# One core, sixteen batches in a pipeline: a layer norm moved one period on, tanh issued behind the gate matmul, a piece of A on GpSimd, A^T and B^T turned by DMA

## Chip, core and metric

The kernel runs on one core of one Trainium2 chip. The metric is the device time of one execution in microseconds, and the number that counts is the median of several executions. The engines are TensorE (PE, its weight loads are listed as PEld), VectorE (DVE), ScalarE (ACT), GpSimd (POOL) and SyncE (SP), which in this kernel only issues DMAs.

## The reference

The input x has 16 batches of 256 tokens of 128 features. One transformer layer is computed: an attention over a window of 128 tokens with 16 heads of 8 features, then a gated feed-forward part whose operands are rounded to a 4-bit grid in blocks of 16, each with a residual and a layer norm.

```
g = x @ Wg.T + bg ;  v = x @ Wv.T + bv                  # 16 heads of 8
corr = (g_i . g_j) / (|g_i| |g_j| + 1e-8) * m           # m: window mask
corr = (corr + 1) / 2
denom = mean_j(corr) + 0.5
fitness = 1 / (denom * sum_i(1 / denom))
attn = softmax(corr * fitness_i, masked)
x = layernorm(x + (attn @ v) @ Wo.T + bo)
gate, up = q(x) @ q(w_gate).T, q(x) @ q(w_up).T         # q: to a 4-bit grid, blocks of 16
h = silu(gate) * up
x = layernorm(x + q(h) @ q(w_down).T)
```

## The kernel before

All five engines run programs written out by hand, each a loop over a period number t from -3 to 20. The engines meet by semaphores only, and each engine takes its instructions strictly in the order written. In one period t every engine does a piece of work for several batches: the genes and values of batch t+3, the normalised genes and the fitness of batches t+2 and t+1, the scores and exponentials of batch t, the rest of its attention with t-1, the first layer norm and the rounding of x of batch t-2, the gate, up and hidden part of t-2 and t-3, and the down projection and second layer norm of t-4.

Scores of a batch come from two half-precision matrices. A16 holds the normalised genes gh in four pieces per head: the rounded value twice and the remainder (the low piece) twice; B16 holds the genes times fitness (Bf) in the same way. Both lie with tokens on the 128 partitions and must be turned so that the pieces lie on partitions; the results are AT and BT, two buffers each.

- GpSimd writes the rounded halves of B16 (L516) and A16 (L525), VectorE the low halves: `low_B` (L1175) and, for A, L1344.
- TensorE turns them with `turn16` (L811), eight 128x128 transposes through PSUM bank WB for each matrix, and ScalarE copies the bank to AT (L617) and BT (L635).
- `scores` (L745, L751) of eight pairs of heads fill PSUM banks S; ScalarE's `exps` (L568) empty them; a pair waits for the exponentials of the pair before. `values` (L772) multiplies the result with v.
- `window_sums` (L847) needs A16 complete, and gives VectorE the row sums (L1377 to L1390, the last of them `rden`); `fitness_sums` (L858) sums `rden` on TensorE, and `project` (L796) follows it there.
- `gate_up` (L804, L805) multiplies first for the gate, then for the up part. `tanh` on ScalarE (L599) waits for the semaphore that the up matmul raises; VectorE then does `gate` (L1181) and `up` (L1187).
- The second layer norm of batch t-4 is made in period t: `residual_2` (L1168) and the statistics `st2` (L1148) and `mv2` (L1154) on VectorE between the rounding steps `hm` (L1199), `rstd` on GpSimd (L501 to L506) between its two products `hq` (L495), the result `yo` on ScalarE (L574) at the end of the period.
- `newton` on GpSimd (L471 to L478) finds 1/|g| in twelve small steps at the start of its period; the first layer norm's `rstd` follows behind B16's copy.
- SP issues per period one load of x turned (L378), one load of x (L382) and one store (L385), 128 KB each.

## Time and profile before

| what | value |
|---|---|
| median of 3 executions | 354.0 us (353.38 to 361.8) |
| the profiled execution | 353.57 us |
| its span in the trace | 351.9 us |
| busy: PE, DVE, ACT, POOL | 280.9, 266.8, 236.8, 176.2 us |
| mean granted TensorE clock | 0.935 |

The profiled execution stands for the runs. 1.67 us of it lie outside the span, ahead of the first instruction and behind the last. No engine is busy all the time, so the page's table of busy shares alone doesn't say what sets the time; the chain of work that ended last and the engines' own lists in order of time do.

### The profile page before, as it was taken

To read this page: it belongs to the slowest core of one execution; us is meant where nothing else is said; L and a number is where in the kernel's file an instruction comes from. 1 tells how busy PE (TensorE), PEld (TensorE's weight loads), DVE (VectorE), ACT (ScalarE), POOL (GpSimd) and SP (SyncE) were. 2 spreads that over 40 slices of the span, in tenths; PEclk is the share of its full clock that TensorE was granted. 3 is DMA by queue.
4 is the path that set the end of the run, shared out by engine and by line. 5 is a ranking of instruction groups with operands and counts; after the bars stand their busy time and mean duration, and the time that the engine had idled before them with its cause. 6 is when DMAs were issued, how large, how long until landed. Compare 5 with 4: busy or idle time off the path is not lost.

```text
span 351.9 us, 13497 instructions
## 1 busy us (share of the span) xinstructions
PE 280.9 (80%) x5268; PEld 190.1 (54%) x5268; DVE 266.8 (76%) x777; ACT 236.8 (67%) x531; POOL 176.2 (50%) x457
## 2 busy tenths in 40 slices
PE   5548788887898989898989898889888989762731
PEld 3334455655565656565656565657564656531521
DVE  3752856578989798989888888989898989867631
ACT  2044655777787979797979797979796988531330
POOL 6463330626455656566565656565655244351351
PEclk9999955999999999999999999999999999986765
DMA  4100000101010101011010101010001010000000
GB/s 129 30 3 31 17 4 1 34 2 34 5 30 12 40 14 37 16 35 30 21 32 21 31 18 35 17 33 2 23 13 32 5 34 4 15 10 4 19 15 19
DMA packets 12422, 7.93 MB, mean 23 GB/s; under 512 B 1026, under 2 KB 12356, under 8 KB 12356
## 3 DMA queue, kind: packets, MB, share of 16 engines
q1 hardware_dynamic: 12356, 7.03, 7.0%
q8 instruction: 43, 0.70, 0.8%
q14 instruction: 23, 0.19, 0.2%
HBM read 4.93 MB, written 2.10 MB: 20 GB/s over the span
## 4 chain that ended last, share of the span: by engine, by line
DVE 34%; PE 30%; issue 17%; ACT 9%; POOL 8%; DMA 1%; SPq 0%; POOLq 0%; ACTq 0%; DVEq 0%
PE OT L772 8%; ACT Pm L568 4%; PE WC L804 3%; DVE xn L1230 3%; PE WB L811 3%; DVE hm L1199 3%; PE WA L823 2%; PE S L745 2%; PE WD L805 2%; DVE A L1344 2%; ACT y L574 2%; DVE st L1148 2%; PE WB L796 2%; DVE xn L1238 2%; DVE xn L1240 2%
## 5 line engine op out<-in xcount | busy, mean ns | idle before, releaser
L568 ACT ACTIVATE Pm<-S 128x384 f32<-128x384 f32 x256 | 111.4, 490 | 36.2 <-PE S L751 36.2
L772 PE MATMUL OT<-Pm,gv 128*32 128x256 f32 (+1 forms) x1024 | 58.0, 346 | 0.0
L495 POOL TENSOR_TENSOR hq<-hm,hs 128x352 f32<-128x352 f32 x32 | 25.6, 801 | 62.7 <-DVE hm L1199 62.7
L745 PE MATMUL S<-BT,AT 32*32 32x160 f16 (+4 forms) x2048 | 40.7, 223 | 14.9 <-ACT Pm L568 13.7
L745 PEld LDWEIGHTS S<-BT,AT 32*32 32x32 f16 x2048 | 17.8, 88 | 46.8 <-ACT Pm L568 32.0
L772 PEld LDWEIGHTS OT<-Pm,gv 128*32 128x32 f32 x1024 | 27.6, 113 | 20.9 <-issue 6.2
L804 PE MATMUL WC<-wguT,xaT 128*128 128x352 f32 x58 | 26.3, 536 | 6.6 <-ACT xaT L656 6.2
L751 PE MATMUL S<-mask,ident 32*32 32x96 f16 x1024 | 31.1, 206 | 0.0
L912 PE MATMUL WD<-wdT,hqT 128*128 128x128 f32 (+1 forms) x192 | 26.8, 292 | 1.8 <-ACT hqT L628 1.8
L1181 DVE SCALAR_TENSOR_TENSOR hh<-th,WC 128x352 f32<-128x352 f32 x29 | 14.5, 499 | 17.4 <-ACT th L599 17.4
L588 ACT ACTIVATE hu<-hn,off 128x352 f32<-128x352 f32 x32 | 18.8, 591 | 12.5 <-POOL hn L489 12.5
L912 PEld LDWEIGHTS WD<-wdT,hqT 128*128 128x128 f32 (+1 forms) x192 | 23.8, 199 | 3.4 <-ACT hqT L628 2.4
L489 POOL TENSOR_TENSOR hn<-h,hrn 128x352 f32<-128x352 f32 x32 | 24.7, 793 | 1.3
L1199 DVE SCALAR_TENSOR_TENSOR hm<-hu,hn 128x352 f32<-128x352 f32 x32 | 22.0, 687 | 3.7 <-ACT hu L588 3.7
L823 PE MATMUL WA<-wgv,xT 128*128 128x256 f32 x64 | 21.5, 469 | 4.0 <-DMA bgrow<-bg_dram 3.8
L599 ACT ACTIVATE th<-WC 128x352 f32<-128x352 f32 x29 | 13.4, 463 | 16.6 <-PE WD L805 16.6
L805 PE MATMUL WD<-wguT,xaT 128*128 128x352 f32 x58 | 23.1, 482 | 0.0
L504 POOL TENSOR_TENSOR rstd<-ve,mhalf 128x2 f32<-128x2 f32 x32 | 22.9, 715 | 0.0
L574 ACT ACTIVATE yo<-y,nb,rstd 128x128 f32<-128x128 f32 x32 | 14.0, 489 | 10.7 <-POOL nb L506 10.7
L617 ACT ACTIVATE AT<-WB 128x1024 f16<-128x1024 f16 x16 | 16.4, 1023 | 6.9 <-PE WB L811 5.7
L501 POOL TENSOR_SCALAR ve<-mv 128x2 f32<-128x2 f32 x32 | 9.8, 306 | 20.3 <-DVE mv L1154 19.0
L471 POOL TENSOR_TENSOR nt<-seed 128x32 f32<-128x32 f32 x15 | 4.0, 265 | 28.1 <-DVE seed L1116 28.1
(165 smaller groups left out, 694.7 us busy)
## 6 DMA issues: line engine op xcount, KB each, us to landing
xT<-x_turned_dram SPq DMA_DIRECT2D x16, 128.0 KB, 2.3
x_res<-x_dram SPq DMA_DIRECT2D x16, 128.0 KB, 2.2
out_dram<-yo SPq DMA_DIRECT2D x16, 128.0 KB, 2.1
wf<-w_down_dram SPq DMA_DIRECT2D x1, 176.0 KB, 2.5
wgv<-wgv_dram SPq DMA_DIRECT2D x1, 128.0 KB
wf<-w_gate_dram SPq DMA_DIRECT2D x1, 128.0 KB, 2.1
wf<-w_up_dram SPq DMA_DIRECT2D x1, 128.0 KB, 2.1
woT<-wo_dram SPq DMA_DIRECT2D x1, 64.0 KB
```

The lines of the kernel that those rows point to most:

```text
L489: pool.tensor_tensor(b3(hn[:, k]), b3(h[:, k]), bc(hrn[:, k], QB), ALU.mult).then_inc(s_hn, 1)
L495: pool.tensor_tensor(b3(hq[:, k, 0:I]), b3(hm[:, k]), bc(hs[:, k], QB), ALU.mult).then_inc(s_hq, 1)
L504: pool.tensor_tensor(r[:, :], ve[:, :], mhalf[:, 0:NT], ALU.pow).then_inc(s_out, 1)
L568: act.activation(Pm[:, group % PR, hd % 4, :], S[:, (H * x + hd) % 3, 0:SCW], ACT.Exp, scale=1.0 / ZS).then_inc(s_exp, 1)
L745: pe.matmul(S[k0:k0 + KG, bank, at:at + n], AT[r:r + 32, x % 2, c, q:q + KG], BT[r:r + 32, x % 2, c, q:q + n], start=(kt == 0), stop=False)
L751: i = pe.matmul(S[k0:k0 + KG, bank, 0:SCW].rearrange("p (b c) -> p b c", c=P)[:, :, k0:k0 + KG], ident16[m:m + KG, m:m + KG], near[m:m + K ...
L772: i = pe.matmul(OT[VP * g:VP * (g + 1), T - (q1 - q0):T], gv_flat[:, at:at + VP], Pm[:, (GROUPS * x + c) % PR, g, q0:q1], start=(kt == 0 a ...
L804: pe.matmul(g, lhs, wguT[:, 0:I], start=True, stop=True)
L805: pe.matmul(u, lhs, wguT[:, I:2 * I], start=True, stop=True).then_inc(s_gu, 1)
L823: pe.matmul(WA[:, k * 2 * D:(k + 1) * 2 * D], xT[:, (t + 3) % 2, k * P:(k + 1) * P], wgv[:, :], start=(k == 0), stop=False)
L912: i = pe.matmul(WD[:, k * D:(k + 1) * D], hqT[0:kn, k, n * P:(n + 1) * P], wdT[0:kn, n, :], start=(n == 0), stop=(n == 2))
L1199: dve.scalar_tensor_tensor(out=hm[:, k], in0=hu[:, k], scalar=ROUND, in1=hm[:, k] if step else hn[:, k], op0=ALU.max, op1=op).then_inc(s_h ...
```

## The change

Four things are changed. The second layer norm's statistics, `rstd` and result of batch x are now made in period x+5 for the batches below 12 (`late`); `residual_2` stays in period x+4, and y2 has two buffers. `tanh` waits for a new semaphore that the gate matmul raises, and `up` waits for the up matmul's own. A's low piece is computed by GpSimd, after the two products `hn` and ahead of the moved `rstd`. `turn16` and the two ScalarE copies are gone: SP issues for each of A and B two transposing DMAs from SBUF to SBUF, 128x512 half-precision elements each, behind the low piece and the end of the scores that read the same buffer. TensorE's `scores` wait for the DMA's semaphores, and so do GpSimd's writes of the next A16 and B16.

```diff
-        y2 = sb("y2", [P, NT, D])
+        y2 = sb("y2", [P, 2, NT, D])
...
+        def late(x):
+
+            return x < B - 4
...
+            def turned(src, dst, x, s_done):
+
+                for n in range(NT):
+                    sp.dma_start(dst[:, x % 2, :, n * P:(n + 1) * P],
+                                 src[:, n * H:(n + 1) * H].rearrange("p h r d -> p (h r d)"),
+                                 transpose=True).then_inc(s_done, 16)
...
+                for x in (t - 6, t - 5):
+                    if live(x) and late(x) == (x == t - 6):
+                        sp.wait_ge(s_yo, NT * x + NT)
+                        sp.dma_start(ov[x], yo[:, x % 2]).then_inc(st_o[x % 2], 16)
+
+                if live(t + 1):
+
+                    need(sp, s_sc, H * t)
+                    sp.wait_ge(s_Blo, t + 2)
+                    turned(B16, BT, t + 1, s_B)
+                if live(t + 2):
+
+                    need(sp, s_sc, H * (t + 1))
+                    sp.wait_ge(s_Alo, t + 3)
+                    turned(A16, AT, t + 2, s_A)
...
-                    need(pool, s_A, t + 2)
+                    need(pool, s_A, 32 * (t + 2))
                     pool.tensor_copy(A16[:, :, 0:2, :], twice(gh)).then_inc(s_Ahi, 1)
...
                 if live(t - 3):
                     h_over_scale(t - 3, 0)
                     h_over_scale(t - 3, 1)
+                if live(t + 2):
+
+                    pool.wait_ge(s_Ahi, t + 3)
+                    pool.tensor_tensor(A16[:, :, 2:4, :], twice(gh), A16[:, :, 0:2, :], ALU.subtract).then_inc(s_Alo, 1)
+                if live(t - 5) and late(t - 5):
+                    norm_2(t - 5)
+                if live(t - 3):
                     h_times_scale(t - 3, 0)
...
             def tanh(x, k):
-                act.wait_ge(s_gu, NT * x + k + 1)
+                act.wait_ge(s_gate, NT * x + k + 1)
...
-                if live(t + 1):
-                    act.wait_ge(s_A, t + 2)
-                    need(act, s_sc, H * t)
-                    act.activation(AT[:, (t + 1) % 2].rearrange("p c t -> p (c t)"), WB16, ACT.Copy).then_inc(s_AT, 1)
...
                 if p == 0:
-                    pe.wait_ge(s_AT, x + 1)
-                    pe.wait_ge(s_BT, x + 1)
+                    pe.wait_ge(s_A, 32 * (x + 1))
+                    pe.wait_ge(s_B, 32 * (x + 1))
...
-                pe.matmul(g, lhs, wguT[:, 0:I], start=True, stop=True)
+                pe.matmul(g, lhs, wguT[:, 0:I], start=True, stop=True).then_inc(s_gate, 1)
...
+                if live(t - 5) and late(t - 5):
+                    sums_2(t - 5)
+                    aggr_2(t - 5)
                 if live(t - 3):
                     gate(t - 3, 1)
...
-                if live(t + 2):
-                    dve.wait_ge(s_Ahi, t + 3)
-                    need(dve, s_A, t + 2)
-                    dve.tensor_tensor(A16[:, :, 2:4, :], twice(gh), A16[:, :, 0:2, :], ALU.subtract).then_inc(s_Alo, 1)
```

GpSimd, from A's rounded halves (`A<-gh`) over the hidden part's products `hn` and `hq` to the first step of the next period's `newton` (`nt<-seed`), in the kernel before:

```order
L525 CAST A<-gh 128x32x16
L485 TENSOR_SCALAR hrn<-hr 128x44
L489 TENSOR_TENSOR hn<-h,hrn 128x352 x2
L495 TENSOR_TENSOR hq<-hm,hs 128x352
L501 TENSOR_SCALAR ve<-mv 128x2
L502 TENSOR_SCALAR nm<-mv 128x2
L504 TENSOR_TENSOR rstd<-ve,mhalf 128x2
L506 TENSOR_TENSOR nb<-nm,rstd 128x2
L495 TENSOR_TENSOR hq<-hm,hs 128x352
L471 TENSOR_TENSOR nt<-seed 128x32
```

The same place in the changed kernel:

```order
L551 CAST A<-gh 128x32x16
L506 TENSOR_SCALAR hrn<-hr 128x44
L510 TENSOR_TENSOR hn<-h,hrn 128x352 x2
L562 TENSOR_TENSOR A<-gh,A 128x32x16
L522 TENSOR_SCALAR ve<-mv 128x2
L523 TENSOR_SCALAR nm<-mv 128x2
L525 TENSOR_TENSOR rstd<-ve,mhalf 128x2
L527 TENSOR_TENSOR nb<-nm,rstd 128x2
L516 TENSOR_TENSOR hq<-hm,hs 128x352 x2
L492 TENSOR_TENSOR nt<-seed 128x32
```

The four steps of `rstd` moved ahead of both `hq`, A's low piece is new ahead of them, and the two `hq` now stand together.

VectorE, from the last step of rounding x (`xm`) over A's low piece, the rounding of the hidden part (`hm`) and the second norm (`y<-y,WD`, `st`, `mv`) to the sizes of the genes (`n`), in the kernel before:

```order
L1243 TENSOR_TENSOR xm<-xn,xs 128x256
L1344 TENSOR_TENSOR A<-gh,A 128x32x16
L1199 SCALAR_TENSOR_TENSOR hm<-hu,hn 128x352
L1168 TENSOR_TENSOR y<-y,WD 128x256
L1199 SCALAR_TENSOR_TENSOR hm<-hu,hm 128x352
L1148 BN_STATS st<-y 128x6 x2
L1199 SCALAR_TENSOR_TENSOR hm<-hu,hn 128x352
L1154 BN_AGGR mv<-st 128x2 x2
L1199 SCALAR_TENSOR_TENSOR hm<-hu,hm 128x352
L1110 TENSOR_REDUCE n<-gsq 128x32
```

The same place in the changed kernel:

```order
L1263 TENSOR_TENSOR xm<-xn,xs 128x256
L1219 SCALAR_TENSOR_TENSOR hm<-hu,hn 128x352
L1187 TENSOR_TENSOR y<-y,WD 128x256
L1219 SCALAR_TENSOR_TENSOR hm<-hu,hm 128x352
L1219 SCALAR_TENSOR_TENSOR hm<-hu,hn 128x352
L1219 SCALAR_TENSOR_TENSOR hm<-hu,hm 128x352
L1122 TENSOR_REDUCE n<-gsq 128x32
```

A's low piece left this engine, and the second norm's `st` and `mv` left this stretch; for the batch before they now stand earlier in the period, between `Bf` and the second `gate`.

ScalarE, from the copy of the values (`OTs`) to the first layer norm's result (`y`), in the kernel before:

```order
L599 ACTIVATE th<-WC 128x352
L568 ACTIVATE Pm<-S 128x384 x2
L581 ACTIVATE OTs<-OT 128x256
L617 ACTIVATE AT<-WB 128x1024
L568 ACTIVATE Pm<-S 128x384 x2
L574 ACTIVATE y<-y,nb,rstd 128x128 x2
```

The same place in the changed kernel:

```order
L637 ACTIVATE th<-WC 128x352
L601 ACTIVATE Pm<-S 128x384 x2
L614 ACTIVATE OTs<-OT 128x256
L601 ACTIVATE Pm<-S 128x384 x2
L607 ACTIVATE y<-y,nb,rstd 128x128 x2
```

The copy of AT left the line between the exponentials; the copy of BT, later in the period, left it in the same way.

## Rows read from the trace of the kernel before

**Rows 1.** Chain that ended last, in order of time: start us, us, what; whole trace.

```profile
93.56 0.36 DVE rden L1390
...
185.67 0.57 PE WB L811 x8
...
187.18 0.87 ACT Pm L568 x2
...
193.00 0.68 DVE A L1344
...
198.06 0.36 DVE rden L1390
...
267.51 0.36 DVE rden L1390
```

**Rows 2.** ScalarE's instructions: start us, us, line, [idle before <-who ended it], one period.

```profile
184.64 0.46 ACT L599 ACTIVATE th<-WC 128x352 f32<-128x352 f32 x1 [0.40 <-PE WD L805]
...
185.79 0.39 ACT L581 ACTIVATE OTs<-OT 128x256 f32<-128x256 f32 x1
...
188.03 0.88 ACT L574 ACTIVATE y<-y,nb,rstd 128x128 f32<-128x128 f32 x2
```

**Rows 3.** GpSimd's instructions, same columns and period.

```profile
187.95 0.61 POOL L525 CAST A<-gh 128x512 f16<-128x512 f32 x1
...
194.96 0.79 POOL L495 TENSOR_TENSOR hq<-hm,hs 128x352 f32<-128x352 f32 x1 [4.48 <-DVE hm L1199]
196.45 0.30 POOL L501 TENSOR_SCALAR ve<-mv 128x2 f32<-128x2 f32 x1 [0.70 <-DVE mv L1154]
...
197.91 0.79 POOL L495 TENSOR_TENSOR hq<-hm,hs 128x352 f32<-128x352 f32 x1
198.66 0.24 POOL L471 TENSOR_TENSOR nt<-seed 128x32 f32<-128x32 f32 x1
```

**Rows 4.** VectorE's instructions, same columns and period.

```profile
185.14 0.52 DVE L1181 SCALAR_TENSOR_TENSOR hh<-th,WC 128x352 f32<-128x352 f32 x1 [1.08 <-ACT th L599]
...
193.60 0.52 DVE L1199 SCALAR_TENSOR_TENSOR hm<-hu,hn 128x352 f32<-128x352 f32 x1
...
194.80 0.48 DVE L1148 BATCH_NORM_STATS2 st<-y 128x6 f32<-128x128 f32 x2
195.19 0.94 DVE L1199 SCALAR_TENSOR_TENSOR hm<-hu,hn 128x352 f32<-128x352 f32 x1
196.05 0.23 DVE L1154 BATCH_NORM_AGGREGATE mv<-st 128x2 f32<-128x6 f32 x2
...
197.73 0.17 DVE L1116 TENSOR_SCALAR seed<-seed 128x32 int32<-128x32 int32 x1
```

**Rows 5.** TensorE's matmuls, same columns and period.

```profile
193.22 0.41 PE L937 MATMUL WC<-identf,xm 128*128 128x128 f32 x2 [0.38 <-DVE xm L1243]
...
197.44 0.23 PE L751 MATMUL S<-mask,ident 32*32 32x96 f16 x8
198.56 0.38 PE L858 MATMUL WA<-rden,onesf 128*128 128x32 f32 x2 [0.89 <-DVE rden L1390]
```

**Rows 6.** SP's loads of x, line 382: times of issue (min/median/max ns), landing.

```profile
L382 SPq DMA_DIRECT2D x_res<-x_dram x16: 367/368/441, 12.4 to 286.9; - x16
...
DMA to landing us min/median/max: 2.0/2.2/3.5
```

**Rows 7.** DMA queue, page part 3: packets, MB, share of 16 engines.

```profile
q1 hardware_dynamic: 12356, 7.03, 7.0%
```

**Rows 8.** Start of the kernel, instructions of VectorE, TensorE and GpSimd.

```profile
20.78 0.85 DVE L1344 TENSOR_TENSOR A<-gh,A 128x512 f16<-128x512 f32 x1 [0.71 <-POOL A L525]
...
22.53 0.82 PE L847 MATMUL WB<-A,win 128*128 128x128 f16 x6
...
24.70 0.75 POOL L441 MEMSET gv<- 128x782 f32 x1
```

**Rows 9.** Busy us by engine in a stretch: PE, PEld, DVE, ACT, POOL, granted clock, DMA.

```profile
40.00:60.00 20.00, 15.75 (x291) 10.24 (x291) 12.68 (x25) 10.58 (x23) 4.95 (x15) 0.57 0.01 3
```

More of the change, by code:

```diff
@@ L188, in layer @@
         WD = ps("WD", [P, 512])
-        WB16 = WB[:, :].bitcast(F16)
         ld_w = sem("ld_w")
@@ L234, in layer @@
         s_xqT = sem("s_xqT")
+        s_gate = sem("s_gate")
         s_gu = sem("s_gu")
@@ L506, in rstd, with norm_2 @@
                 pool.tensor_tensor(nb[:, :], nm[:, :], r[:, :], ALU.mult).then_inc(s_out, 1)
+            def norm_2(x):
+                need(pool, s_yo, NT * x)
+                rstd(x, mv2, ve2, rstd2, nm2, nb2, s_ln2, 5 * x + 5, s_rs2)
             for t in range(FIRST, LAST + 1):
@@ L535, in _ @@
                     rstd(B - 1, mv1, ve1, rstd1, nm1, nb1, s_ln1, 5 * B, s_rs1)
-                if live(t - 4):
-                    rstd(t - 4, mv2, ve2, rstd2, nm2, nb2, s_ln2, 5 * (t - 4) + 5, s_rs2)
+                if live(t - 4) and not late(t - 4):
+                    norm_2(t - 4)
                 if live(t - 3):
@@ L594, in apply_1, with apply_2 @@
                 ln_apply(y, rstd1, nb1, y1[:, (t - 2) % YR], s_y1)
+            def apply_2(x):
+                act.wait_ge(s_rs2, 4 * x + 4)
+                need(act, st_o[x % 2], 16 * (x // 2))
+                ln_apply(y2[:, x % 2], rstd2, nb2, yo[:, x % 2], s_yo)
             def tanh(x, k):
-                act.wait_ge(s_gu, NT * x + k + 1)
+                act.wait_ge(s_gate, NT * x + k + 1)
                 need(act, s_hh, NT * x + k - 1)
@@ L679, in _ @@
                 exps(t, 7)
-                if live(t - 4):
-                    act.wait_ge(s_rs2, 4 * (t - 4) + 4)
-                    need(act, st_o[t % 2], 16 * ((t - 4) // 2))
-                    ln_apply(y2, rstd2, nb2, yo[:, t % 2], s_yo)
+                if live(t - 5) and late(t - 5):
+                    apply_2(t - 5)
+                if live(t - 4) and not late(t - 4):
+                    apply_2(t - 4)
             with act.If(flag_set(act)):
@@ L803, in gate_up @@
                 lhs = xaT[:, T + k * P:T + (k + 1) * P]
-                pe.matmul(g, lhs, wguT[:, 0:I], start=True, stop=True)
+                pe.matmul(g, lhs, wguT[:, 0:I], start=True, stop=True).then_inc(s_gate, 1)
                 pe.matmul(u, lhs, wguT[:, I:2 * I], start=True, stop=True).then_inc(s_gu, 1)
-            def turn16(src, s_done):
-                for c in range(4):
-                    for n in range(NT):
-                        i = pe.transpose(WB16[:, c * T + n * P:c * T + (n + 1) * P], src[:, n * H + 4 * c:n * H + 4 * c + 4].rearrange("p h r d -> p (h r d)"),
-                                         ident16[:, :])
-                i.then_inc(s_done, 1)
             def genes_values(t):
@@ L877, in _ @@
                 values(t - 1, 3)
-                if live(t + 1):
-                    after_last(pe, (t - 2, s_ln1, 5 * (t - 2) + 1), (t + 1, s_fit, 8 * (t + 1) + 1))
-                    pe.wait_ge(s_Alo, t + 2)
-                    if t == -1:
-                        pe.wait_ge(c_pool, 9)
-                    turn16(A16, s_A)
                 scores(t, 2)
@@ L894, in _ @@
                 scores(t, 3)
-                if live(t + 1):
-                    pe.wait_ge(s_AT, t + 2)
-                    pe.wait_ge(s_Blo, t + 2)
-                    turn16(B16, s_B)
                 if live(t - 1):
@@ L1148, in ln_sums, with sums_2, aggr_2 @@
                     dve.bn_stats(st[:, k, :], yy[:, k, :]).then_inc(s, 1)
+            def sums_2(x):
+                ln_sums(x, s_ln2, y2[:, x % 2], st2)
+            def aggr_2(x):
+                need(dve, s_rs2, 4 * x)
+                ln_aggr(x, s_ln2, st2, mv2)
             def ln_aggr(x, s, st, mv):
@@ L1185, in up @@
                 dve.wait_ge(s_hh, NT * x + k + 1)
+                dve.wait_ge(s_gu, NT * x + k + 1)
                 need(dve, s_hn, NT * (x - 1) + k + 1)
@@ L1281, in _ @@
                     residual_2(t)
-                    ln_sums(t - 4, s_ln2, y2, st2)
-                    ln_aggr(t - 4, s_ln2, st2, mv2)
+                    sums_2(t - 4)
+                    aggr_2(t - 4)
                 if t < 1 and live(t + 1):
@@ L1289, in _ @@
                         gene_size(2, k)
+                if live(t - 5) and late(t - 5):
+                    sums_2(t - 5)
+                    aggr_2(t - 5)
                 if live(t - 3):
@@ L1356, in _ @@
                     round_h(t - 3, 0, 1)
-                if live(t - 4) and t != B + 1:
-                    ln_sums(t - 4, s_ln2, y2, st2)
+                if live(t - 4) and t != B + 1 and not late(t - 4):
+                    sums_2(t - 4)
                 if t == B:
@@ L1364, in _ @@
                     round_h(t - 3, 1, 0)
-                if live(t - 4) and t != B + 1:
-                    ln_aggr(t - 4, s_ln2, st2, mv2)
+                if live(t - 4) and t != B + 1 and not late(t - 4):
+                    aggr_2(t - 4)
                 if live(t - 3):
```

21 lines of the change are left out of this document (6 added, 15 removed).

## Prediction

> **What bounds the kernel now.** I read the chain that ended last first, then each engine's list in order of time over one period. From batch 4 on the chain meets VectorE's `rden` at 93.56 us and, ten periods later, at 267.51 us [rows 1], so a period is 173.95 / 10 = 17.40 us, and half of the span is this one period repeated. Within it the chain goes round one ring. `rden` ends (198.06 + 0.36 us), TensorE sums it and goes on in its order through project, scores, gate, values and the eight transposes of A (185.67 us), ScalarE copies AT and gets to the exponentials at 187.18 us [rows 1], makes y (the first layer norm) at 188.03 us [rows 2], and from there VectorE works almost without a pause until the next `rden`, with A's low piece at 193.00 us on the way [rows 1]. So three things count: the stretch from the transposes to y, VectorE's stretch from y to `rden`, and whether TensorE, which waits only 0.89 us for `rden` and 0.38 us for `xm` [rows 5], is ready earlier too. GpSimd waits 4.48 us for VectorE's `hm` [rows 3] and is not full.
>
> **The turn and the copies.** The values before the turn are done at 185.67 us and the next exponentials start at 187.18 us [rows 1], 1.51 us later. Without turn and copy TensorE makes the next scores at once; ScalarE still has `OTs` to do, until 185.79 + 0.39 = 186.18 us [rows 2]. The exponentials can start there, 1.0 us earlier, and y behind them. But y also needs GpSimd's `nb`, which stands behind `newton` on that engine, and `newton` began at 198.66 us behind the second `hq` [rows 3].
>
> **The second norm a period behind.** On GpSimd its four steps took from 196.45 to the `hq` at 197.91 us, 1.46 us [rows 3], with VectorE's fresh `mv` ahead of them. Moved ahead of the first `hq`, where 4.48 us were idle, they cost nothing; if that cover were gone they would cost those 1.46 us again. `newton` is then held only by its seed, which VectorE finishes at 197.73 + 0.17 = 197.90 us [rows 4], so it starts 198.66 - 197.90 = 0.76 us earlier. That is less than 1.0, so y and all behind it come 0.75 us earlier. On VectorE, `st` and `mv` take 0.39 us (194.80 to 195.19) and up to 0.23 us [rows 4] out of the ring, 0.6 in all. They go in front of the second `gate`, which waited 1.08 us for tanh [rows 4]; ScalarE's yo no longer waits for GpSimd, and nothing else hangs on it.
>
> **tanh behind the gate matmul.** ScalarE was idle for 0.40 us ahead of tanh, waiting for the up matmul [rows 2]; it was busy before that, so 0.40 is all that can be won. `gate` then waits 1.08 - 0.40 = 0.68 us, which the moved `st` and `mv` fill with their 0.6. Nothing of it adds to the ring; it pays for the move.
>
> **A's low piece on GpSimd.** VectorE loses 193.60 - 193.00 = 0.60 us of work [rows 1, 4]. For GpSimd I take the product `hq`, 0.79 us for 352 columns [rows 3]: 512 columns give 0.79 x 512 / 352 = 1.15 us, in the idle 4.48 us, and sooner than VectorE had it, since it comes right behind `hn`. It isn't quite free: while `hq` ran (194.96 to 195.75 us) VectorE's `hm` from 195.19 us took 0.94 us where the same step took 0.52 at 193.60 us [rows 3, 4], so 0.56 us side by side cost 0.42. A's low piece will stand beside VectorE's rounding of x, at 0 to 1.15 x 0.42 / 0.56 = 0.86 us. I take 0.4, the middle, because the steps there have one or two operands and the dear row is one of two.
>
> **The sum of a period.** VectorE's way round the ring gets shorter by 0.75 + 0.6 + 0.6 - 0.4 = 1.55 us (1.1 with the full 0.86, 1.95 with none). TensorE's way from `xm` to `fitness_sums` is unbroken in its list; it can come earlier by the 0.75 us of `xm` and the 0.89 us for which it waited [rows 5], 1.64. Both limits meet: 1.55 us a period, and what is late next is both at once.
>
> **Transposing DMAs.** No row shows one. Bounded from below by plain loads of the same 128 KB on the same queue: 0.37 us to issue one, 2.2 us to landing [rows 6], a pair in 2.6 us. Bounded from above by moving every element by itself: 12,356 packets took 7.0% of 16 engines [rows 7], 0.070 x 16 x 351.9 / 12,356 = 32 ns each, so 65,536 elements on 16 engines would take 131 us a transfer. I take about 4 us a pair: size, queue and engines are those of the load, only the order of writing differs. A's pair may start when the period's scores end, 197.44 + 0.23 = 197.67 us [rows 5], and the first to wait for it is GpSimd's next rounding of A, at 187.95 + 17.42 = 205.37 us in the old rhythm [rows 3]: 7.7 us of room, 6.1 in a period shorter by 1.55. `hn` and `hq`, and behind them `hu` and `hm`, are queued behind that copy. B's pair has longer, from ahead of the rounding of x to the next period's first scores. On SP the x load, its wait for the residual and the store stand between the pairs, and each is asked for a period ahead. So at 4 us it is hidden.
>
> The Trainium skill, page DMA: Bandwidth & Descriptors, section Latency and other measured facts, gives transposing DMAs an effective 261 GB/s; 128 KB would take an estimated 0.5 us beyond the fixed part, which would leave the sum as it is. No run here shows it yet.
>
> **The start, the rest and the end.** At the start GpSimd's list has A's low piece of the second batch behind the bias rows and a memset that ends at 24.70 + 0.75 = 25.45 us; with 1.15 us it is done at 26.6, where VectorE was done at 20.78 + 0.85 = 21.63 us. `window_sums`, at 22.53 us before, waits for it [rows 8]: 4.1 us later, 4.3 with the first batch's low piece ahead of `newton`. The DMA of the first B, some 4 us, hides behind that wait. One period on VectorE skips such a wait (0.71 us) and piece (0.6), so 3.0 us are left as a loss. From 40 to 60 us the granted clock was 0.57 [rows 9], most of the stretch at the lower of the two levels; the turns there take about twice as long, and without them and the copy I count 2.0 us won (an estimate). The two periods ahead of the ten and the two behind carry part of the work: 1.1 us each, 4.4. The tail keeps the old order for the last four batches; tanh gives an estimated 0.5.
>
> Together: 10 x 1.55 + 4.4 + 2.0 + 0.5 - 3.0 = 19.4 us. The profiled execution took 353.57 us, 351.9 in the span and 1.67 around it; that is 0.4 below the median of the runs, 354.0, so it stands for them. 353.6 - 19.4 = 334.2, **334 us**, 5.6% less.
>
> **Rivals.**
>
> *The transposes are slow (ends slower).* Place: GpSimd's rounding of A, behind A's pair. It decides from 6.1 us a pair on; the gain is gone at 6.1 + 1.55 = 7.7 us, and some 14 periods pay whatever is above. With 11 us a pair it is 14 x 3.3 = 46 us more than before, 400 us; with the upper bound the kernel would be many times slower. For it: no row prices the operation, and the same words are written out of order. Against it: size and queue. 0.19.
>
> The Trainium skill, page VectorE: DVE Perf Modes, section The three transpose paths, speaks against the change: 128x128 half-precision elements in 390 ns on TensorE and 1309 ns by DMA, and TensorE where PSUM will do. A pair is eight such blocks; one after another they would be an estimated 10.5 us and bring this rival about. The trace has TensorE's eight in 0.57 us [rows 1], and shows nothing of the DMA.
>
> *y is no earlier.* If GpSimd's first norm stays where it was (its `newton` starts earlier, but `Bf` or the gates hold it), only VectorE's own 0.6 + 0.6 - 0.4 = 0.8 us remain: 8 + 2.5 + 2.0 + 0.5 - 3.0 = 10 us, 344 us. 0.13.
>
> *Contention and the start eat it.* With 0.86 us beside GpSimd and no earlier y a period gains 0.35, and the start may cost 5 us and lengthen the stretch at the lower clock: 3.5 + 2 - 5 + 1 = 1.5 us won, 352 us. 0.10.
>
> **How the numbers follow.** The forecast has 0.58, for 323 to 340: its lower end has no contention and a TensorE that closes its other small waits (2.1 a period, 21 + 6 + 3 + 1 - 2 = 29 us), its upper end 1.1 a period. Two per cent, about what measuring this kernel can tell from no change, is 7 us: faster below 346.5, slower above 360.6. Faster 0.58 + 0.13 = 0.71, same 0.10, slower 0.19. The range goes up into the third rival and a little of the first: 323 to 356 leaves out some 0.03 below and 0.17 above.
>
> **What would show it.** In the changed profile: a period of about 15.85 us between one `rden` and the next; no AT or BT group on ScalarE; DMA pairs done within 6 us, and GpSimd's A copy not waiting for a DMA; `newton` right behind the seed; `hq` twice in a row; xm to `rden` on VectorE shorter by some 1.2 us; `window_sums` at the start near 27 us. The prediction is wrong if scores or the A16 and B16 copies wait for the transposes, if SP's queue is still busy when B is ready, or if VectorE's rounding of x stretches by the whole length of GpSimd's new piece.

## The result, and the profile after

The changed kernel takes 349.86 us (median of 6 runs, 347.44 to 351.01) against 353.71 us before: a ratio of 0.9862, with an interval from 0.9829 to 0.9895 (the two medians alone give 0.989). That is faster, as forecast, but by 1.4% where 5.6% was forecast: within 2%, to which the prediction gave 0.10. It lies outside 323 to 340, to which the forecast gave 0.58, and inside 323 to 356 only because that range was widened for the rivals. The profiled execution took 347.44 us, 345.2 of it in the span, at a mean granted clock of 0.961; the five other runs had 0.936 to 0.946 and took 347.8 to 351.0. Runs over 1.5% longer than the shortest of their kernel are left out of all ratios; the profiled executions of two experiments (A's low piece back on VectorE, second norm in its old period) are such runs, and their periods are read from 110 us on.

VectorE's list of the kernel after, with the start of each instruction in us, its duration, and in brackets its wait, answers to [rows 1, 4]. The first and the last line bound the ten periods, the rest is one undisturbed period:

```profile
94.43 0.35 DVE L1409 RECIPROCAL rden<-den 128x32 f32<-128x32 f32 x1
...
230.05 0.35 DVE L1409 RECIPROCAL rden<-den 128x32 f32<-128x32 f32 x1
...
237.85 0.42 DVE L1244 TENSOR_REDUCE xmax<-y 128x16 f32<-128x256 f32 x1 [0.44 <-ACT y L607]
...
239.86 0.98 DVE L1253 TENSOR_SCALAR xu<-xn 128x256 int32<-128x256 int32 x1
...
242.33 0.42 DVE L1263 TENSOR_TENSOR xm<-xn,xs 128x256 f32<-128x256 f32 x1
...
243.87 0.52 DVE L1219 SCALAR_TENSOR_TENSOR hm<-hu,hn 128x352 f32<-128x352 f32 x1
244.43 0.99 DVE L1219 SCALAR_TENSOR_TENSOR hm<-hu,hm 128x352 f32<-128x352 f32 x1
...
246.00 0.32 DVE L1125 TENSOR_SCALAR seed<-n 128x32 int32<-128x32 int32 x1
...
246.89 0.35 DVE L1409 RECIPROCAL rden<-den 128x32 f32<-128x32 f32 x1
...
263.31 0.35 DVE L1409 RECIPROCAL rden<-den 128x32 f32<-128x32 f32 x1
```

The same list of the kernel before, one period, for the split of the ring:

```profile
180.64 0.35 DVE L1390 RECIPROCAL rden<-den 128x32 f32<-128x32 f32 x1
...
188.95 0.42 DVE L1224 TENSOR_REDUCE xmax<-y 128x16 f32<-128x256 f32 x1 [0.45 <-ACT y L574]
...
190.95 0.23 DVE L1233 TENSOR_SCALAR xu<-xn 128x256 int32<-128x256 int32 x1
...
192.65 0.42 DVE L1243 TENSOR_TENSOR xm<-xn,xs 128x256 f32<-128x256 f32 x1
```

The ring can be cut at two places, the start of `xmax` (the first step of rounding x, which waits for y) and the end of `xm` (the last step). Before: 188.95 - 180.64 = 8.31 us from `rden` to `xmax`, 4.12 to the end of `xm`, 4.99 to the next `rden` (198.06), 17.42 in all. After: 7.80, 4.90 and 4.14, 16.84 in all. So y comes 0.51 earlier, VectorE's stretch behind `xm` is 0.85 shorter, and the rounding of x between them is 0.78 longer. The forecast had 0.75, 1.2 and 0.4. In this period the first `xu`, a step in between, accounts for it: 0.98 us in place of 0.23. In five of the ten periods it does so alone. In the other five the first `xu` takes 0.60 us and the second step, also called `xu`, 0.91, and from `xmax` to the end of `xm` it is again 4.89 to 4.91 us.

GpSimd's list of the kernel after, same columns and period, answers to [rows 3]:

```profile
229.96 0.24 POOL L492 TENSOR_TENSOR nt<-seed 128x32 f32<-128x32 f32 x1 [0.53 <-DVE seed L1128]
...
236.25 0.66 POOL L527 TENSOR_TENSOR nb<-nm,rstd 128x2 f32<-128x2 f32 x1
236.86 0.60 POOL L551 CAST A<-gh 128x512 f16<-128x512 f32 x1
...
239.34 1.34 POOL L562 TENSOR_TENSOR A<-gh,A 128x512 f16<-128x512 f32 x1
...
244.04 1.00 POOL L516 TENSOR_TENSOR hq<-hm,hs 128x352 f32<-128x352 f32 x1 [1.69 <-DVE hm L1219]
245.50 0.78 POOL L516 TENSOR_TENSOR hq<-hm,hs 128x352 f32<-128x352 f32 x1 [0.46 <-DVE hm L1219]
```

A's low piece ends at 239.34 + 1.34 = 240.68 us and the held `xu` at 240.84; `hq` ends at 245.04 and the last `hm` at 245.42. One of the other five periods, GpSimd's line and then VectorE's:

```profile
206.31 1.20 POOL L562 TENSOR_TENSOR A<-gh,A 128x512 f16<-128x512 f32 x1
```

```profile
206.42 0.41 DVE L1353 TENSOR_TENSOR attn<-WA,orec 128x256 f32<-128x256 f32 x1
206.75 0.91 DVE L1256 TENSOR_SCALAR xu<-xu 128x256 f32<-128x256 f32 x1
```

`attn`, which reads PSUM, takes its usual 0.41 us wholly inside the piece, and the `xu` behind it, 0.28 us without the piece, ends 0.15 us after the piece does.

`newton` (line 492) does start right behind the seed now, as foreseen, and nothing waits for a DMA ahead of the rounding of A at 236.86.

The transposing DMAs of A in the kernel after (issue times min/median/max in ns, landing in us), and the page's line on the queue, answer to [rows 6, 7]:

```profile
L379 SPq DMA_TRANSPOSE AT<-A x32: 1190/1267/2624, 13.9 to 264.6; - x32
...
DMA to landing us min/median/max: 2.4/2.5/4.5
```

```profile
q1 hardware_dynamic: 47172, 15.43, 20.4%
```

A pair takes 2.5 us of SP's time (up to 3.9 in some periods) and by these medians lands 1.27 + 2.5 = 3.8 us after it begins; 4 was taken.

TensorE's list of the kernel after shows the new place of its waiting, ahead of the turn of `xm` on line 949 ([rows 5] had 0.38 us here):

```profile
57.41 1.91 PE L845 MATMUL WA<-wgv,xT 128*128 128x256 f32 x4
...
89.88 0.66 PE L949 MATMUL WC<-identf,xm 128*128 128x128 f32 x2 [1.80 <-DVE xm L1263]
...
124.52 0.41 PE L949 MATMUL WC<-identf,xm 128*128 128x128 f32 x2 [1.82 <-DVE xm L1263]
124.77 1.03 PE L845 MATMUL WA<-wgv,xT 128*128 128x256 f32 x4
...
191.36 0.41 PE L949 MATMUL WC<-identf,xm 128*128 128x128 f32 x2 [1.67 <-DVE xm L1263]
191.61 1.57 PE L845 MATMUL WA<-wgv,xT 128*128 128x256 f32 x4
...
242.90 0.41 PE L949 MATMUL WC<-identf,xm 128*128 128x128 f32 x2 [1.18 <-DVE xm L1263]
243.15 1.03 PE L845 MATMUL WA<-wgv,xT 128*128 128x256 f32 x4
```

Behind the wait at 191 us the same matmul group took 1.57 us in place of 1.03. Its windows (busy us by engine, then granted clock, DMA share, GB/s) show the clock beside it: it went from the higher level, 2.4 GHz, to the lower one, 1.2 GHz, for some 3.5 us, and the period from 195.45 us on took 17.76 us. Not every wait of that length does this: behind 1.82 us at 124.52 the group took its 1.03 us.

```profile
190.00:191.50 1.50, 0.14 (x1) 0.17 (x2) 1.43 (x4) 0.34 (x1) 1.17 (x3) 1.00 0.00 0
191.50:193.00 1.50, 1.50 (x7) 1.02 (x7) 1.47 (x5) 0.60 (x1) 0.41 (x1) 0.65 0.02 5
193.00:195.40 2.40, 2.40 (x24) 1.30 (x22) 2.40 (x7) 0.87 (x2) 1.41 (x3) 0.51 0.02 7
```

### The profile page after: what moved, and what is told of

Read it like the earlier page. It is cut to its first block and busy times, and to the rows that moved or that the text cites. A ratio compares the mean times of both kernels' runs of the same rounds, so it can differ in the third digit from the quotient of the medians.

```text
span 345.2 us, 12985 instructions
## 1 busy us (share of the span) xinstructions
PE 267.1 (77%) x5012; PEld 176.8 (51%) x5012; DVE 271.8 (79%) x761; ACT 208.9 (61%) x499; POOL 198.8 (58%) x473
## 5 line engine op out<-in xcount | busy, mean ns | idle before, releaser
L803 PE MATMUL OT<-Pm,gv 128*32 128x256 f32 (+1 forms) x1024 | 59.4, 353 | 0.0
L516 POOL TENSOR_TENSOR hq<-hm,hs 128x352 f32<-128x352 f32 x32 | 28.1, 879 | 32.6 <-DVE hm L1219 32.6
L924 PE MATMUL WD<-wdT,hqT 128*128 128x128 f32 (+1 forms) x192 | 28.0, 300 | 6.4 <-ACT hqT L662 6.2
L845 PE MATMUL WA<-wgv,xT 128*128 128x256 f32 x64 | 22.9, 495 | 3.7 <-DMA bgrow<-bg_dram 3.4
L621 ACT ACTIVATE hu<-hn,off 128x352 f32<-128x352 f32 x32 | 17.5, 597 | 11.5 <-POOL hn L510 11.5
L1219 DVE SCALAR_TENSOR_TENSOR hm<-hu,hm 128x352 f32<-128x352 f32 x32 | 23.2, 725 | 0.5
L949 PE MATMUL WC<-identf,xm 128*128 128x128 f32 x32 | 7.1, 305 | 18.7 <-DVE xm L1263 18.6
L562 POOL TENSOR_TENSOR A<-gh,A 128x512 f16<-128x512 f32 x16 | 20.2, 1260 | 0.2
L1219 DVE SCALAR_TENSOR_TENSOR hm<-hu,hn 128x352 f32<-128x352 f32 x32 | 17.0, 531 | 3.7 <-ACT hu L621 3.7
L687 ACT ACTIVATE xaT<-WC 128x512 f32<-128x512 f32 (+1 forms) x16 | 9.1, 570 | 16.9 <-issue 14.7
```

The source lines that it names most:

```text
L516: pool.tensor_tensor(b3(hq[:, k, 0:I]), b3(hm[:, k]), bc(hs[:, k], QB), ALU.mult).then_inc(s_hq, 1)
L803: i = pe.matmul(OT[VP * g:VP * (g + 1), T - (q1 - q0):T], gv_flat[:, at:at + VP], Pm[:, (GROUPS * x + c) % PR, g, q0:q1], start=(kt == 0 a ...
L845: pe.matmul(WA[:, k * 2 * D:(k + 1) * 2 * D], xT[:, (t + 3) % 2, k * P:(k + 1) * P], wgv[:, :], start=(k == 0), stop=False)
L924: i = pe.matmul(WD[:, k * D:(k + 1) * D], hqT[0:kn, k, n * P:(n + 1) * P], wdT[0:kn, n, :], start=(n == 0), stop=(n == 2))
L1219: dve.scalar_tensor_tensor(out=hm[:, k], in0=hu[:, k], scalar=ROUND, in1=hm[:, k] if step else hn[:, k], op0=ALU.max, op1=op).then_inc(s_h ...
```

## Experiments

The theory after this reading: VectorE's `xu` is held, that is, it stands still, until GpSimd's new instruction ends, and that eats the gain of taking A's low piece off VectorE. The rivals: the transposing DMAs slow the engines; or the loss lies in TensorE's clock after its longer waits. The kernels below are the changed kernel with one edit each, if not said otherwise. Times are compared by their ratio to runs of the kernel before on the same chip in the same hour (0.9862 for the change; 0.01 is 3.5 us).

### Each part taken back alone

**A's low piece back on VectorE**, behind `xm` as before.

```diff
-                    pool.tensor_tensor(A16[:, :, 2:4, :], twice(gh), A16[:, :, 0:2, :], ALU.subtract).then_inc(s_Alo, 1)
...
+                    dve.tensor_tensor(A16[:, :, 2:4, :], twice(gh), A16[:, :, 0:2, :], ALU.subtract).then_inc(s_Alo, 1)
```

> The changed kernel with A's low piece back on VectorE at its old place; the other three parts stay. In the changed kernel the second step of rounding x on VectorE (xu, 0.23 us before) takes 0.98 us in the same microseconds in which GpSimd computes A's low piece, and it ends when that piece ends. Theory (VectorE held until GpSimd's piece is done): xu falls back to 0.23 to 0.28 us, the way from xmax to xm from 4.48 to about 3.7 us, the way from xm to rden grows by 0.6 us; a period gets some 0.15 us shorter, 16.7 us, and the start some 2.7 us, because window_sums no longer waits for GpSimd's list: about 345 us where the changed kernel has 350. Rival (the transposing DMAs of B, in flight in the same microseconds, slow VectorE): xu stays at 0.98 us, the period becomes 16.84 + 0.6 = 17.4 us, and the time 353 us.

Measured: 343.66 us, ratio 0.9694 (0.9650 to 0.9737), faster than both kernels and the fastest that computes everything. VectorE's list in a period of 16.67 us:

```profile
240.84 0.42 DVE L1240 TENSOR_REDUCE xmax<-y 128x16 f32<-128x256 f32 x1 [0.44 <-ACT y L603]
...
242.84 0.22 DVE L1249 TENSOR_SCALAR xu<-xn 128x256 int32<-128x256 int32 x1
...
244.55 0.43 DVE L1259 TENSOR_TENSOR xm<-xn,xs 128x256 f32<-128x256 f32 x1
244.89 0.69 DVE L1363 TENSOR_TENSOR A<-gh,A 128x512 f16<-128x512 f32 x1
...
249.71 0.35 DVE L1409 RECIPROCAL rden<-den 128x32 f32<-128x32 f32 x1
```

`xu` is back at 0.22 us, `xmax` to `xm` at 4.14; from `xm` to `rden` it is 4.73, so the piece costs VectorE 0.6 here and had cost it 0.76 from GpSimd. In most of the other periods the first `xu` takes 0.60 us, held by the end of `hn` (at 142.13 us with 0.45 us of `hn` left), and `xmax` to `xm` 4.25. Periods from 132 us on are 16.5 to 17.0 us but the shorter last one. The start is better too: the second `rden` stands at 25.82 us (28.42 in the changed kernel, 24.72 before), the third at 43.21 (44.81 and 42.14). One of the four parts of the change was a loss.

**The turns back on TensorE, the copies on ScalarE**, the other three parts kept.

```diff
-                    turned(A16, AT, t + 2, s_A)
...
+                    turn16(A16, s_A)
...
+                    act.activation(AT[:, (t + 1) % 2].rearrange("p c t -> p (c t)"), WB16, ACT.Copy).then_inc(s_AT, 1)
...
```

The lines shown are A's; B's are put back in the same way.

> The changed kernel with A and B turned by TensorE and copied by ScalarE as before, no transposing DMA; the other three parts stay. Theory (VectorE held by GpSimd): xu stays slow, near 0.98 us, with no DMA in flight, and since y comes 0.5 us later behind the AT copy the period is about 17.3 us; 355 us. Rival (DMA traffic slows VectorE): xu is back at 0.23 us, the period about 16.6 us, and the time 344 us.

Measured: 354.22 us, ratio 1.0022 (0.9963 to 1.0081), periods of 17.04 to 17.19 us from 115 us on but the shorter last one. It also tells the rivals apart, since no transposing DMA is in flight here and the hold is the same. VectorE, then GpSimd:

```profile
193.82 0.98 DVE L1264 TENSOR_SCALAR xu<-xn 128x256 int32<-128x256 int32 x1
```

```profile
193.31 1.34 POOL L547 TENSOR_TENSOR A<-gh,A 128x512 f16<-128x512 f32 x1
```

So the DMAs do not slow `xu`. (In the periods of 17.19 us the first `xu` takes 0.22 us and the steps ahead of it are held, and `xmax` to `xm` is 4.85 to 4.87.) Turning by DMA is worth 0.35 us a period and (1.0022 - 0.9862) x 354 = 5.7 us in all, since with it y comes 0.39 us earlier (8.19 us from `rden` to `xmax` here, 7.80 with the DMAs).

**The second norm in its old period.**

```diff
-            return x < B - 4
+            return False
```

> The changed kernel with the second layer norm in its old period for all batches; the other three parts stay. If moving it was worth what the changed trace shows (newton 0.69 us earlier, st and mv 0.55 us out of the stretch from xm to rden), the period grows by 0.5 to 1.1 us to 17.4 to 17.9 us and the time to 355 to 364 us. Rival (the move is worth nothing, since VectorE is held anyway): the period stays within 0.2 us of 16.84 and the time at 350 us.

Measured: 356.1 us, ratio 0.9969 (0.9919 to 1.002), periods of 17.40 us (8.13, 4.90 and 4.37). Moving the norm is worth 0.56 us a period, 0.33 of it an earlier y and 0.23 behind `xm`; by the ratios it is 3.8 us, with the two intervals only just apart.

**tanh behind the up matmul, as before.**

```diff
-                act.wait_ge(s_gate, NT * x + k + 1)
+                act.wait_ge(s_gu, NT * x + k + 1)
```

> The changed kernel with tanh waiting for the up matmul again; the other three parts stay. In the changed trace the second gate starts 0.08 us after its tanh, and VectorE waits 0.44 us for y a little later. If the 0.47 us by which tanh comes later is swallowed by that wait, the period grows by 0.1 us at most and the time is 350 to 352 us; if it is not, the period is 17.3 us and the time 356 us.

Measured: 357.55 us, ratio 1.01 (1.0064 to 1.0136), a miss: (1.0100 - 0.9862) x 354 = 8.4 us, more than was expected of any part. The undisturbed period is 16.83 us, so the ring doesn't see tanh's place, as forecast. But five periods took 17.4 to 19.3 us, and from 267.82 us to the end it took 87.5 us (81.9 in the changed kernel). TensorE's list and its windows at one of them:

```profile
109.79 0.66 PE L949 MATMUL WC<-identf,xm 128*128 128x128 f32 x2 [1.75 <-DVE xm L1263]
110.25 1.91 PE L845 MATMUL WA<-wgv,xT 128*128 128x256 f32 x4
```

```profile
104.00:108.00 4.00, 4.00 (x86) 3.08 (x84) 3.86 (x11) 3.58 (x10) 2.99 (x4) 1.00 0.57 70
108.00:112.00 4.00, 2.25 (x8) 1.69 (x8) 3.86 (x9) 1.29 (x3) 1.12 (x2) 0.72 0.02 2
112.00:116.00 4.00, 4.00 (x79) 2.47 (x77) 2.08 (x8) 2.53 (x7) 2.04 (x7) 0.86 0.00 0
```

TensorE was busy 2.25 of 4 us, waited 1.75 us for `xm`, and ran at the lower clock behind it.

### What the hold depends on

**Half of the piece.** From the second batch on only the first 128 rows of A's low piece are computed; the kernel leaves the other half out.

```diff
-                    pool.tensor_tensor(A16[:, :, 2:4, :], twice(gh), A16[:, :, 0:2, :], ALU.subtract).then_inc(s_Alo, 1)
+                    m = NT * H if t == -2 else H
+                    pool.tensor_tensor(A16[:, 0:m, 2:4, :], twice(gh)[:, 0:m], A16[:, 0:m, 0:2, :],
+                                       ALU.subtract).then_inc(s_Alo, 1)
```

> The changed kernel with A's low piece computed, from the second batch on, for the first 128 rows only (the other half keeps the piece of the first batch): GpSimd's subtraction is half as wide, 0.65 us in place of 1.34, and nothing else is changed. Theory (VectorE's xu is held until GpSimd's subtraction ends): the held xu goes from 0.98 us to 0.3 us or less, xmax to xm from 4.90 us to 4.2, the period from 16.84 to about 16.2 us, and the time to about 343 us. Rival 1 (the transposing DMAs or a fixed cost of sharing make xu slow): xu stays near 0.9 us and the period above 16.7, 349 us. Rival 2 (the hold moves on to the next operation, or TensorE's own work of the period takes over as the bound): xu short, but the period 16.5 or more, 346 us.

Measured: 341.03 us, ratio 0.9608 (0.9575 to 0.9641), periods of 16.37 us (7.82, 4.41 and 4.14). GpSimd, then VectorE:

```profile
233.76 0.86 POOL L563 TENSOR_TENSOR A<-gh,A 128x256 f16<-128x256 f32 x1
```

```profile
234.28 0.49 DVE L1255 TENSOR_SCALAR xu<-xn 128x256 int32<-128x256 int32 x1
```

GpSimd's piece is 0.48 us shorter, `xu` 0.49. `xu` isn't at the 0.3 us expected, because it still starts 0.34 us before the shorter piece ends. Nothing on VectorE was edited, and nothing else in the ring moved. That makes the hold the cause of the longer rounding of x.

**attn, which reads PSUM, ahead of the first `xu`.**

```diff
-                    quant_x(t - 2, 4)
...
                     dve.tensor_tensor(attn[:, :, :], o[:, :, 0:HD], bc(orec[:, :], HD), ALU.mult).then_inc(s_attn, 1)
...
+                    quant_x(t - 2, 4)
```

> The changed kernel with one swap on VectorE: attn, which reads PSUM, goes ahead of the first xu, which reads SBUF alone. The work is the same, GpSimd's A low stays where it is. Theory (only VectorE operations on SBUF are held while GpSimd's subtraction runs; an operation that reads PSUM runs through): attn's 0.41 us runs beside the subtraction for nothing and the held xu is shorter by as much; in the periods with a held first xu (0.98 us, period 16.84) xmax to xm goes from 4.90 to about 4.5 us and the period to 16.45; in those with 0.60 and 0.91 us it gains 0.1 to 0.2. Time 344 to 347 us. Rival (the piece's price is its own length, wherever it stands): 4.90 and 16.84 stay, 349.9 us.

Measured: 351.47 us, ratio 0.992 (0.9879 to 0.996), no gain. In four of the ten periods `xu` took 0.52 us and the period 16.68 us, 0.16 better than 16.84 where 0.4 was expected. In the others `xu` now starts with GpSimd's piece and is held for the whole of it. GpSimd, then VectorE, in such a period:

```profile
190.57 1.16 POOL L562 TENSOR_TENSOR A<-gh,A 128x512 f16<-128x512 f32 x1
```

```profile
190.26 0.42 DVE L1351 TENSOR_TENSOR attn<-WA,orec 128x256 f32<-128x256 f32 x1
190.60 1.27 DVE L1253 TENSOR_SCALAR xu<-xn 128x256 int32<-128x256 int32 x1
```

Here `attn` ran its usual 0.42 us beside the tail of `hn`, as it did at 206.42 us beside the piece, so this operation, which reads PSUM, isn't held. But a swap that only shifts the start of the held operation can lengthen the hold as well as shorten it.

**`hq` only behind the last `hm`**, with A's low piece back on VectorE.

```diff
             def h_times_scale(x, k):
+                if k == 0:
+                    pool.wait_ge(s_hr, 2 * NT * (x + 1))
```

> A's low piece back on VectorE (343.66 us, undisturbed periods of 16.53 and 16.67 us), and GpSimd starts the first half of hq only when VectorE has written the last hm. Theory (hm's last step takes 0.99 us in place of 0.52 because GpSimd's hq runs beside it): hm takes 0.52 us, xm to rden goes from 4.74 to 4.3 us, the period to about 16.2 us, and the time to about 339 us. Rival (the hold moves to the seed and the sums that follow hm, or the turned hq comes 0.8 us later to TensorE and holds the down product): the period stays at 16.6 us or more, 343 us or more.

Measured: 345.27 us, ratio 0.9722 (0.9673 to 0.9771), against 0.9694 with the piece back alone: no gain, a miss. VectorE's list:

```profile
173.57 0.53 DVE L1217 SCALAR_TENSOR_TENSOR hm<-hu,hm 128x352 f32<-128x352 f32 x1
...
174.67 0.33 DVE L1123 TENSOR_SCALAR seed<-n 128x32 int32<-128x32 int32 x1
...
175.25 0.49 DVE L1126 TENSOR_SCALAR seed<-seed 128x32 int32<-128x32 int32 x1
```

The last `hm` lost its hold (0.99 to 0.53 us), and the second seed took 0.49 us in place of 0.17; the first had 0.32 without this edit too. Of 0.46 us, 0.17 arrived at `rden` (4.57 from 4.74): the rival, that the hold moves on, was right. Beside the same two `hq` (174.18 to 175.71 us) `gw`, which reads PSUM, from 174.34 us and the reduction `rs` from 174.92 us kept their 0.41 us each.

### The room of the DMAs

**Each pair of transposing DMAs twice**, the first into a spare buffer.

```diff
+                if spares[0]:
+                    sp.wait_ge(s_spare, 16 * spares[0])
+                for n in range(NT):
+                    sp.dma_start(spare[:, :, n * P:(n + 1) * P],
+                                 src[:, n * H:(n + 1) * H].rearrange("p h r d -> p (h r d)"),
+                                 transpose=True).then_inc(s_spare, 16)
+                spares[0] += NT
```

> The changed kernel with every pair of transposing DMAs preceded by a like pair into a spare buffer that nothing reads. The pair took 2.5 us of SP's time and landed some 3.8 us after its start. Theory (the transposes are hidden and neither slow VectorE nor GpSimd): xu, A low and hq keep their durations; the pair for A now lands about 2.5 to 3.8 us later, at 247 to 248.3 us in the period in which it landed at 244.5 and TensorE first needs it at 247.0, so TensorE waits 0 to 1.3 us for it, beside a ring that VectorE and GpSimd set: 349 to 356 us. Rival (transposing DMAs slow the engines' SBUF operations): xn, xu, A low or the norm's steps get longer by tenths in each period, VectorE's part of the period grows although no engine waits for a DMA, 355 us or more.

Measured: 360.94 us, ratio 1.018 (1.0125 to 1.0236), longer than the theory's upper end, and not by TensorE's wait that I had named. (The landing at 244.5 us in the expectation was misread: in the changed kernel A's pair begins at 230.64 and lands at about 234.4 us, and GpSimd's rounding at 236.86 is the first behind it.) GpSimd's waits (total us, times, longest) and VectorE's `hm`:

```profile
POOL A L562 <- DMA AT<-A: 30.8, 14, 3.9
```

```profile
218.20 0.52 DVE L1230 SCALAR_TENSOR_TENSOR hm<-hu,hn 128x352 f32<-128x352 f32 x1
```

GpSimd's rounding of A waits 2.2 us a period for the old A to be read, where it waited 0.3 us once in the changed kernel; that is the place that the forecast had named for slow transposes. It shifts A's low piece onto the second and third step of the rounding (an `xn` of 1.26 us), while unheld operations keep their durations with twice the DMAs in flight (`hm` 0.52 us). So DMAs cost the engines nothing until the buffer's room is used up. What was left of it is 236.86 - 230.64 - 3.8 = 2.4 us, and the spare pair ahead of A's took 2.5 us of SP's time and up to 3.75.

### TensorE's clock

**Six unread turns of a constant** fill TensorE's wait for `xm`, from period t = 4 on.

```diff
+                    for k in range(6 if 4 <= t <= B else 0):
+                        pe.transpose(WC[:, T + (k % 2) * P:T + (k % 2 + 1) * P], identf[:, :], identf[:, :])
                     pe.wait_ge(s_xq, 9 * (t - 2) + 9)
```

> The changed kernel, and in each period from the seventh on TensorE turns a constant six times into the half bank that the turn of xm overwrites, right before it waits for xm; nothing reads these turns. Two turns took 0.41 us and three 0.55 us in the changed kernel, so six take about 1 us and lie in its wait of 1.2 to 1.8 us for xm. Theory (after that wait TensorE runs at its lower clock for a stretch in some periods, and this is why one period took 17.76 us and others 17.15 and 16.94 where the undisturbed one takes 16.84): no matmul group of the period is longer than in the undisturbed period after 95 us, all periods from there are 16.6 to 16.9 us, the time is about 346 us and the runs lie within 1.5 us of each other. Rival (the clock does not follow from that wait): the longer periods stay, 349 to 351 us, or more where the turns end after xm.

Measured: 348.6 us, ratio 0.9807 (0.9781 to 0.9832), runs within 1.55 us. All periods from 129 us on are 16.85 to 16.97 us but the shorter last one, so the stretched ones are gone there. But the two periods behind 94 us took 18.20 and 17.02 us, where the changed kernel had 17.15 and 16.94, so the expectation was met only in part.

**The same one period sooner**, to cover the wait of 1.80 us at 89.66 us that was still there.

```diff
-                    for k in range(6 if 4 <= t <= B else 0):
+                    for k in range(6 if 3 <= t <= B else 0):
```

> The changed kernel with the six unread turns in TensorE's wait for xm one period sooner than in the first such run: that one (348.6 us) still waited 1.80 us for xm at 89.66, the granted clock was 0.56 and 0.50 from 88 to 94 us, and its next period took 18.20 us. Theory (that wait brought the lower clock): no period from 94 us on over 17.0, and about 347 us. Rival (the clock falls there for another reason, such as the load before): the period of 18.2 us stays, 348.6 us or more.

Measured: 347.23 us, ratio 0.978 (0.9718 to 0.9842). The long period only moved: 18.25 us from 77.06 us on, and the one after it took 17.17. The granted clock was 0.69 at 72 to 76 us, behind a wait of 1.17 us for `xm`; the changed kernel has such a wait there too (1.16 us) and a clock of 1.00. From 61 to 112 us it took 50.9 us, in the changed kernel 50.1. The theory fits the later periods and falls for this stretch, and the wait alone doesn't decide whether the clock falls.

**The same six turns with tanh behind the up matmul**, from period t = 4 on.

```diff
+                    for k in range(6 if 4 <= t <= B else 0):
+                        pe.transpose(WC[:, T + (k % 2) * P:T + (k % 2 + 1) * P], identf[:, :], identf[:, :])
...
-                act.wait_ge(s_gate, NT * x + k + 1)
+                act.wait_ge(s_gu, NT * x + k + 1)
```

> The same six turns in TensorE's wait for xm, and tanh behind the up matmul as before the change (357.55 us without the turns, with an undisturbed period of 16.83 us, and five of 17.4 to 19.3 us). Theory (tanh's place costs nothing on the ring, and its 7.7 us against the changed kernel were TensorE's clock after longer waits): within 1.5 us of the changed kernel with the turns, about 346 to 348 us. Rival (the late tanh holds up the later stages by itself): 354 us or more, with the turns or without.

Measured: 352.43 us, ratio 0.9934 (0.9898 to 0.9971): above the theory's 346 to 348 us and below the rival's 354. By the ratios the turns give back 5.9 us, but they help the kernel with the early tanh too (0.9807), and 4.5 of the 8.4 us between early and late tanh stay. From 130 us on all periods are 16.8 to 16.9 us but the shorter last one; the period at 77 us took 18.95. So filling the wait takes away 3.9 of the 8.4 us; what the rest is isn't settled.

### Together

**A's low piece on VectorE, `attn` ahead of `xu`, four unread turns** from period t = 3 on: the edits above in one kernel.

> A's low piece back on VectorE (343.66 us), attn ahead of the first xu, and four unread turns in TensorE's wait for xm from the period at 77 us on. Theory: xu is no longer held by the end of hn (0.60 us to about 0.3 in the periods that had it), periods of 16.4 to 16.6 us throughout, and no period stretched by the lower clock after 77 us: 341 to 342.5 us. Rival (VectorE, 95% busy, is the bound and each hold only moves on): 343 to 344 us.

Measured: 344.97 us, ratio 0.9709 (0.9664 to 0.9753), the same as the piece back on VectorE alone (0.9694). `xu` took 0.28 us throughout, as expected, but the periods from 126 us on are 16.5 to 17.3 us but the shorter last one: no gain, as the rival said. In the periods of 16.99 us VectorE waits for y again (7.81 us from `rden` to `xmax`, 7.53 in the one of 16.47); why isn't shown.

## Why the prediction was right in direction and wrong in size

The span became 6.7 us shorter, not 19.4. A period was to lose 1.55 us and in the undisturbed ones lost 0.58: of the 0.97 missing, 0.38 are in the rounding of x, 0.35 behind `xm` and 0.24 ahead of y. Term by term, in the profiled execution, the shortest of the six:

- **What bounds the kernel, and the ring**: right. The ten periods give 173.95 - (263.31 - 94.43) = 5.1 us of the 15.5; 10.4 of the missing 12.7 us are here.
- **A's low piece, the step that failed.** "I take 0.4, the middle" was 0.78, so a step that was to win 0.2 us a period lost 0.18. The piece did free VectorE of 0.60 us (4.73 against 4.14 with it gone), but the `xu` that starts beside it isn't slowed in part, it stands still to the end of the piece. The row that should have been believed was the `hm` of 0.94 us: it was taken as the dear one of two cases, when the cheap one at 193.60 us ran while GpSimd was idle. The prediction's own last line, that it is wrong if the rounding of x stretches by GpSimd's whole piece, comes near: it stretched by the part of the piece that was left when `xu` started. The part thus cost 0.17 us a period (16.84 against the 16.67 shown) and 1.6 us at the start (44.81 against 43.21), and without it the kernel has 343.66 us; these don't make up the whole 5.9 us, and the rest isn't located. Its third rival, contention and the start, came nearest, for the reason it gave but with a gained y.
- **What st, mv and the piece free behind `xm`**: 0.85 of 1.2. The piece gave its 0.60, so `st` and `mv` gave 0.25 of 0.6. One `hm` is held as before (the last, 0.99 us; it was the third, 0.94), and the second `hq`, no longer behind GpSimd's norm, now stands beside the first seed (0.32 us in place of 0.17). That a freed stretch brings the next GpSimd instruction closer wasn't in the sum. Taking the second norm's move back alone cost 0.56 us a period, so the move itself is worth it.
- **y 0.75 earlier**: 0.51 in five of the ten periods, 0.78 (7.53 us from `rden` to `xmax`) in two, and less or nothing in the other three, the stretched ones. `newton` did start at the seed; then `nb` took 0.66 us in the five, beside VectorE's B low, and 0.20 in the two. The mechanism was right, and its size was met where `nb` was short.
- **Transposing DMAs**: right. 3.8 us a pair for 4, hidden; 230.64 us to 236.86 is the room that A's pair had, 6.2 us for the 6.1 forecast, and doubling the pair used it up. What was left out is SP's 1.27 us for each issue (0.37 for a plain load); the ring didn't wait for it (GpSimd's rounding of A waited for a DMA once, 0.3 us).
- **tanh**: right for the ring, 16.84 against 16.83 us. Its worth of 8.4 us in all came outside the undisturbed periods; 3.9 of them go when TensorE's wait is filled, and the rest stays open. The sum had 0.5 for it, in the tail.
- **Start, cold stretch, end**: right. 2.7 us lost for 3.0 (A's low piece of the second batch, at 25.16 us, makes the window sums wait until 26.46), 1.9 won in the period from 42 to 61 us for 2.0, and 2.5 at the end for 2.7.
- **The two periods ahead of the ten**: 2.2 us forecast, nothing won (32.86 and 32.92 us). Behind the wait of 1.80 us at 89.88 the granted clock was 0.69 and 0.88 from 88 to 96 us; the kernel before had 1.00 there. That TensorE waits longer for `xm` in the changed kernel, and that its clock can fall behind that, was no term of the sum.

What stays open: the other runs of the changed kernel took up to 3.6 us more than the profiled one at a lower mean clock, and no trace shows where; what sets the long period between 77 and 112 us, which filling TensorE's wait only moved; and why the clock falls behind some of TensorE's waits and not behind others as long.

## What to carry to other kernels

Moving an elementwise operation from VectorE to GpSimd isn't priced by its own duration but by what VectorE starts beside it. Count, for each long GpSimd instruction on SBUF, the rest of it as lost to a VectorE operation like `xu` or `hm` here that starts meanwhile. Move it beside idle time or what these lists show unheld, `attn` and `gw` (which read PSUM) and the reduction `rs`. Take the parts of a change back one by one: here three were worth 4 to 8 us each and the fourth had eaten 6 of them (they don't add up to the 4.9 us of the whole, since they act on each other). An engine that is no longer the last one waits longer, and behind such a wait TensorE's clock fell in some periods.
